# Last layer: groups of one-hots weighted on ScalarE, a third sum bank; layer 1: other split of the score sums, three groups

## What is computed

```
K_edge = K[src] + 0.2 * rel_w[edge_relations][:, None, :]
scores = einsum('ehd,ehd->eh', Q[dst], K_edge) / D ** 0.5
ex = exp(scores - segment_max(scores, dst)[dst])
w = ex / segment_sum(ex, dst)[dst]
agg = segment_sum(w[:, :, None] * V[src], dst, N)
```

```
support = x @ weight
msgs = support[edge_col] * edge_val[:, None]
out = relu(segment_sum(msgs, edge_row, N))
# mixing: Q, K = elu(x@Wq)+1, elu(x@Wk)+1; KV = einsum(K, v); Z = 1 / (Q . sum(K) + eps)
msg = layernorm((Q KV Z) @ Wm); h = relu([x, msg] @ W1) @ W2; x + layernorm(h)
```

## Time and profile before

| | us |
|---|---|
| median of three runs | 6693.02 |
| the runs | 6693.02, 6673.39, 6698.75 |
| profiled execution | 6705.66 |
| its span | 6703.8 |
| stretch of the scores of layer 1 (2102 to 2950) | 848 |
| stretch of the weighted sums (3017 to 3356) | 339 |
| stretch of the last layer's sums and mixing (5593 to 6345) | 752 |

### The profile page before, as it was taken

One profiled execution on the slowest core, in us unless ns is written; L12 is line 12 of the kernel. 1 busy time (PEld: TensorE's weight loads), 2 busy tenths in 40 slices (PEclk: granted clock), 3 DMA queues, 4 the chain that ended last, 5 costly groups with the idle time before them and its releaser, 6 DMA issues. The chain is left out here.

```text
span 6703.8 us, 72009 instructions
## 1 busy us (share of the span) xinstructions
PE 4507.2 (67%) x18094; PEld 3156.5 (47%) x18094; DVE 3252.3 (49%) x7708; ACT 1396.5 (21%) x5100; POOL 2706.6 (40%) x2773
## 2 busy tenths in 40 slices
PE   0488845557776766647747665688849996777643
PEld 0256523335663433324446533566627774555543
DVE  6235444442016546657751245577752224587722
ACT  0122200003213444431142220000013332111111
POOL 2456656660112555527641210666600004566332
PEclk9988866668887665559968887566679998899866
DMA  4100023231114877756522210444410003222323
GB/s 146 51 2 2 2 81 92 90 89 63 45 45 151 250 229 234 231 143 206 159 75 81 76 40 0 114 113 113 102 40 0 0 0 95 75 85 85 78 91 107
DMA packets 407856, 616.84 MB, mean 92 GB/s; under 512 B 76553, under 2 KB 304285, under 8 KB 407108
## 3 DMA queue, kind: packets, MB, share of 16 engines
q0 software_dynamic: 124448, 324.61, 17.5%
q1 hardware_dynamic: 279908, 284.99, 13.3%
q10 hardware_dynamic: 3154, 3.20, 0.2%
HBM read 475.70 MB, written 137.50 MB: 91 GB/s over the span
## 5 line engine op out<-in xcount | busy, mean ns | idle before, releaser
L837 POOL DMA_INDIRECT m_rows<-support,far_at x440 | 422.1, 959 | 1033.8 <-POOLq L97 750.1
L3296 POOL DMA_INDIRECT g_sc_rows<-keyval,src_at x440 | 437.4, 994 | 495.0 <-ACT g_sc_rows L3280 178.6
L3921 POOL DMA_INDIRECT g_sp_rows<-h,src_at x440 | 444.8, 1011 | 468.3 <-POOLq L97 264.2
L847 PE MATMUL g_sums_bank<-g_sums_rows,g_sums_same 128*125 128x256 f32 x880 | 350.6, 536 | 297.9 <-issue 284.6
L493 POOL DMA_INDIRECT records<-record,place_at x416 | 420.6, 1011 | 282.2 <-issue 119.4
L837 POOL DMA_INDIRECT g_sums_rows<-h,far_at x440 | 416.6, 947 | 234.1 <-issue 115.6
L3969 PE MATMUL g_sp_bank<-g_sp_rows,g_sp_same 128*125 128x264 f32 x880 | 453.8, 616 | 56.4 <-issue 27.9
L3315 PE MATMUL g_sc_pair<-g1q_parts,g_sc_near 125*128 x1320 | 334.8, 385 | 141.8 <-DVE g_sc_rows L3362 84.4
L847 PEld LDWEIGHTS g_sums_bank<-g_sums_rows,g_sums_same 128*125 128x125 f32 x880 | 199.1, 256 | 449.3 <-issue 402.0
L3280 ACT ACTIVATE g_sc_rows<-g_sc_rows 128x64 f32<-128x64 f32 x1320 | 318.1, 242 | 416.2 <-DVE g_sc_rows L3362 309.3
L847 PE MATMUL m_half<-m_rows,m_same 128*125 128x256 f32 x880 | 278.4, 418 | 133.1 <-issue 123.1
(11 more groups left out here) (706 smaller groups left out, 9999.9 us busy)
## 6 DMA issues: line engine op xcount, KB each, us to landing
kept<-g_sc_rows SPq DMA_DIRECT2D x440, 128.0 KB
g_sp_rows<-kept SPq DMA_DIRECT2D x440, 128.0 KB
xnT<-sorted_rows SPq DMA_DIRECT2D x80, 256.0 KB
answer_rows<-f_answer SPq DMA_DIRECT2D x64, 256.0 KB
g_sc_local_in<-local_rows SPq DMA_DIRECT2D x55, 250.0 KB
g_sp_local_in<-local_rows SPq DMA_DIRECT2D x55, 250.0 KB
answer_rows<-zero SPq DMA_DIRECT2D x1, 9856.0 KB
sorted_rows<-zero SPq DMA_DIRECT2D x1, 8192.0 KB
```

Source lines behind the costliest of these rows:

```text
L837: nc.gpsimd.indirect_dma_start(self.rows[:, k, :], None, self.table, bass.IndirectOffsetOnAxis(ap=core.far_at[:, s:s + 1], axis=0)).then_i ...
L847: nc.tensor.matmul(self.halves[s % slots], self.same[:, s % self.RING, :], self.rows[:, s % self.SLOTS, :], start=True, stop=True).then_in ...
L3296: nc.gpsimd.indirect_dma_start(rows[:, k, :], None, table, bass.IndirectOffsetOnAxis(ap=core.src_at[:, s:s + 1], axis=0)).then_inc(gathere ...
L3921: nc.gpsimd.indirect_dma_start(self.rows[:, k, :], None, self.table, bass.IndirectOffsetOnAxis(ap=core.src_at[:, s:s + 1], axis=0)).then_i ...
```

## The change

Three edits.

1. `edge_scores`: ScalarE sums only the odd pairs, 110 of 220, instead of all but every fourth pair, 165. VectorE reduces all even pairs, 110 instead of 55.
2. `weighted_sums`: three buffers of one-hot groups instead of two. The compare of group g+2 is issued after the second step of group g, and two compares stand before the first step.
3. m3: the new class `WeighedSums` takes the place of `Sums`. VectorE makes the one-hots of eight steps in one comparison of 128x1000 without weights (`match`, three groups held, two ahead; the comparison comes before the add of a group's third step). ScalarE multiplies the 125 columns of each step in place by the weight column (`weigh`), twelve steps ahead: twelve at the start, then after its own work of each slot as many as the slot has steps. TensorE waits for the weighting. The ramp is read from SBUF, and its PSUM bank becomes a third bank of sums. The load of the tile numbers moves directly in front of the add of the fifth step of a group.

Nothing else changes. Diff, its core:

```diff
@@ class WeighedSums(Sums), new
+    HELD = 3
+    LEAD = 12
+    def mark(self, s):
+        return self.marks[:, s // GROUP % self.HELD, s % GROUP, :]
+    def multiply(self, pe, s):
+        nc = self.core.nc
+        slots = len(self.halves)
+        pe.wait_ge(self.weighed, s + 1)
+        if s >= slots:
+            pe.wait_ge(self.added, s - slots + 1)
+        pe.wait_ge(self.gathered[s % self.SLOTS], 16 * (s // self.SLOTS + 1))
+        nc.tensor.matmul(self.halves[s % slots], self.mark(s), self.rows[:, s % self.SLOTS, :], start=True, stop=True).then_inc(self.summed, 1)
+    def weigh(self, act, s):
+        nc, core = self.core.nc, self.core
+        if s % GROUP == 0:
+            act.wait_ge(self.matched, s // GROUP + 1)
+        nc.scalar.activation(self.mark(s), self.mark(s), ACT.Copy, scale=core.near_weight[:, s:s + 1]).then_inc(self.weighed, 1)
+    def match(self, v, g):
+        nc, core = self.core.nc, self.core
+        shape = [W, GROUP, P]
+        if g >= self.HELD:
+            v.wait_ge(self.summed, GROUP * (g - self.HELD + 1))
+        nc.vector.tensor_tensor(self.marks[:, g % self.HELD], bcast_mid(core.ramp[:, 0:P], shape),
+                                bcast_last(core.near_local[:, g * GROUP:(g + 1) * GROUP], shape), ALU.is_equal).then_inc(self.matched, 1)
+    def add(self, v, s):
+        nc = self.core.nc
+        g, k = s // GROUP, s % GROUP
+        if k == 2 and g + self.HELD - 1 < GROUPS:
+            self.match(v, g + self.HELD - 1)
+        if k == 4 and g + 1 < GROUPS:
+            self.tiles.load(g + 1)
...
@@ gnn3_mix3
-            sums, mixing = Sums(core, "m3", table, total), Mixing(core, float(N), 1e-6, ahead=2)
+            sums, mixing = WeighedSums(core, "m3", table, total), Mixing(core, float(N), 1e-6, ahead=2)
...
-            halves, ramp = [ph.ps(f"half{k}") for k in range(2)], ph.ps("ramp")
+            halves = [ph.ps(f"half{k}") for k in range(3)]
...
-                for stage, r, _ in slots:
+                for s in range(sums.LEAD):
+                    sums.weigh(act, s)
+                for (stage, r, _), steps in zip(slots, spans):
...
+                    for s in steps:
+                        if s + sums.LEAD < STEPS:
+                            sums.weigh(act, s + sums.LEAD)
@@ edge_scores
-        return pair % 4 != 3
+        return pair % 2 == 1
@@ weighted_sums
-        same = ph.sb("same", [W, 2, GROUP, P])
+        same = ph.sb("same", [W, 3, GROUP, P])
...
+            compare(1)
             for s in range(STEPS):
                 add(s)
-                if s % GROUP == 1 and s // GROUP + 1 < GROUPS:
-                    compare(s // GROUP + 1)
+                if s % GROUP == 1 and s // GROUP + 2 < GROUPS:
+                    compare(s // GROUP + 2)
```

31 lines of the change are left out of this document (25 added, 6 removed).

## The result

The changed kernel takes 6678.4 us (median of 20 runs, 6658.05 to 6687.22) against 6692.5 us of the kernel before (20 runs, 6672.73 to 6705.96): ratio 0.9978, 95% interval 0.9969 to 0.9986, so 14 us or 0.2% faster. The forecast was 50 us. On another chip the same kernel came out at ratio 0.9956 (0.9943 to 0.9970), 30 us. Both intervals lie clear of 1, so the gain is real, but it is smaller than the 0.5% that the prediction took as the least that one measurement can tell. The time is also close to what R2 would give (6680); that is luck, as its parts are not those of R2 (see "Why the prediction was wrong").

A forecast was written before the change was run, and what follows sets the result against it. No engine is busy throughout the three stretches, so only instructions somebody waits for count. Scores -28, weighted sums -1 and last layer -21 sum to -50 us against the 6693.02 us median: 6643 us, range 6575 to 6712.

The forecast's parts named there:

- R2: Rival, score stage: removing the 3.42 us gate only makes another wait longer; -13 us, 6680 us; chance 0.22.
- Scores, -28 forecast: Layer 1 scores: -26 output projection, -11 first part, +9 visible VectorE reduces; -28 us, from -60 to +35.
- the next limit is ScalarE's other copy, L3104: Scores, output projection: copy ends 2494.87 against L3072's start 2495.94, slack 0.9 to 1.1 us; 26 us saved in all.
- Key/value part, -11: Scores, first part: TensorE's waits for copy L3087 shrink 1.7 us in about 6.5 of 12; -11 us.
- Last layer, -21 forecast: Last layer: +5 adds and compares, -6 and -23 third bank, +3 ScalarE's weighting; -21 us.
- 26 x 0.23 = -6: Last layer, key/value part: third bank spares TensorE's third step a 0.23 us wait in 26 slots; -6 us.
- The third bank, -29: Last layer: -6 us in the key/value part, -23 us from L2123 starting 2.1 us earlier in 11 of 13 runs.
- The compare and the adds, +5: Last layer's runs: adds plus compare take 0.74 us a step against 0.67 to 0.68; 0.4 us in 12 runs, +5.
- R1: Rival, last layer: VectorE's busy time is the bound, so 84 us go there; 6580 us; chance 0.10.
- R3: Rival, slower: reduces all visible +37, last-layer add chains +32, third bank brings nothing; 6762 us; chance 0.10.
- R4: Rival, last layer: ScalarE's queue takes back the gain, +43 instead of +3 us; 6683 us; chance 0.06.
- the prediction's own sign (over 10 us): Last layer: copies out of PSUM waiting on a compare, or TensorE on the weighting, over 10 us, shows queue delay.

The follow-up runs named there:

- e16: Kernel before with odd pairs' score sums on ScalarE and the mixing's copy ahead of the preceding pair's eight pieces; ratio 0.9947.
- e17: Kernel before with third bank alone, odd pairs on ScalarE and the mixing's copy before the pieces; ratio 0.9967.
- e12_bank_dve: Kernel before with the last layer's third bank alone (matches stay on VectorE) and all score sums on VectorE; 6596.5 against 6664.6 us, ratio 0.9907.
- e3_groups: Kernel before with only the third group of one-hots in the weighted sums; ratio 0.9992.
- e2_last: Kernel before with only the last layer's change (groups of eight, weighted by ScalarE, third bank); ratio 0.9988.
- e7_two_banks: Kernel before with the last layer's groups of eight weighted by ScalarE, but two banks of sums as before; ratio 1.0023.
- e11: Kernel before with the last layer's groups of eight and third bank, ScalarE's 440 weightings left out; ratio 0.9975.

## Why the prediction was wrong

**Scores, -28 forecast, none in the profile and -11 by the ratios of the split alone.** The step that failed begins with "the next limit is ScalarE's other copy, L3104" and ends with "that is 0.9 to 1.1 us". The end of that copy was reckoned well (2494.87; the like row after ends at 2494.97), but TensorE's arrival there was left where the old gate had put it. With 3.4 us less of waiting in front, TensorE comes earlier and waits for this very copy: 51.9 us in 22 waits, where 1.9 had been (all idle time in front of that product: 55.9 against 19.4). With the old split every second turn of this copy had no pieces ahead, since one of two odd pairs was VectorE's; with the new one all have. On kind B e16 supports it as a cause: with the copy in front of the pieces both gates go and the gain doubles. On kind A it is read from the waits and not shown by an experiment; e17, with the same order, has the stage as long as before. Along with it, 30.3 us less waiting in front of the shift met 37.4 us of reduces, of which 9 were taken as visible, and TensorE waits 19.4 us more for VectorE's multiplications. How much of the reduces is visible stays open: e12_bank_dve has 165 of them more than the kernel before and the shortest score stage of kind A (752.3 us). A reading was wrong too: the wait of 5.50 us was taken to come once in four pairs, but waits of over 4 us stand in front of 33 of the 220 shifts.

**R2** comes nearest: removing the gate only makes another wait longer, 6680 us. It had 0.22; "TensorE itself is the one that idles 3.42 us" argued against it, and that was the mistake: an engine that idles in one wait is not thereby the one that sets the period. That its 6680 fits the measured 6678.4 is luck all the same: R2 has +9 us in the scores and -21 in the last layer, where the parts alone gave -11 and -8.

**Key/value part, -11:** the wait for L3087 fell from 37.2 to 20.8 us, 16 us, as a wait more than forecast, and no gain in the stage's time is seen in the profile.

**Weighted sums, -1:** not contradicted; e3_groups has a ratio of 0.9992 (0.9980 to 1.0003), which can't be told from none.

**Last layer, -21 forecast, -11 between the first and the last add, -8 by the ratio of e2_last.** The term that failed is "26 x 0.23 = -6" of the key/value part: that part got 6 us longer (176.0 to 181.7). The row puts its 0.23 us down to "issue" and to no bank, and the costs of grouping and weighting were reckoned for the runs alone, while it is the key/value part that is longer in every kernel with the weighting (180.0 to 183.8 us against 170.6 to 178.4). In the runs the sum was right, -16 us against -15. The third bank, -29, measured -19 to -21 on kind A with the ramp's share in it: the mechanism right, the gain a third smaller than forecast. The compare and the adds, +5, measured +8.5 (and "0.07 x 440 = +32" beside it is 31); the pitch of 0.64 and the price of 1.19 us were right. Weighting, taken at 0.30 us, 132 us in all: 140.0 us busy, 0.32 each. A single one takes 389 ns, above both bounds, but one begins before the last has ended. By the Trainium skill ("ScalarE: Activation LUTs", section "What ACT_TABLE_LOAD costs") it was 290 ns, an estimate of 128 us from that page; the trace agrees within 10%. Its effect on the others, +3, lies between 3 and 12 us, across chips.

**R1** fell: VectorE's busy share went down by 56 us in the stage, not by 110.9, because match and add had overlapped in their records (0.40 and 0.42 us in a pitch of 0.68), and the last layer lost 11 us, not 84. The rule of the Trainium skill ("Perfetto Trace Analysis", section "Optimizing Scalar/DVE Operations") that grouping helps a saturated engine does not apply with 522 of 752 us busy: e7_two_banks, the grouping with its weighting and without the third bank, is 15 us slower. **R3** had the third bank bring nothing, and it is what brought most. **R4:** TensorE's products show 40.7 us of waits put down to the weighting, which by the prediction's own sign (over 10 us) would speak for R4. But the sign misleads: every product's own weighting had ended at least 6.88 us before, and its wait ended with an add; in e11 without the weighting there is as much idle time (111.7 us). What ScalarE's queue costs by late copies is within the 3 to 12 us above, not 43.

## What to carry to other kernels

A wait that goes is worth only the distance to the next one in the same queue: when a gate in front of TensorE is removed, move TensorE's arrival at every later wait forward by the same time before reading the slack off the old trace. In an engine's fixed order, which short copy stands behind which long block can matter as much as how the blocks are shared out; try the copy that somebody waits for in front. A profile puts a wait for a counter down to whoever raised it last: count which step the waiter needs before believing the name. Grouping small operations pays only if their latency was not already hidden by their neighbours, and a bank that lets the producer go one step further can be had alone (here -21 us, against -8 with the grouping).
